# Attention with a third accumulating transfer per unit, keys loaded in halves, and a new order of work in the unit

## Chip, cores and metric

One core of a Trainium2 chip runs the whole program in one launch. The metric is the device time of the program in microseconds (us); lower is better. Before the change it is 3730.32 us, the median of three runs (3730.3 to 3734.2).

## What is computed

x is 8 x 1024 x 512 in float32. A conditioned transformer block is followed by a conditioned RMS norm:

```python
tp = (silu(time_emb) @ Wt + bt)[:, None, :]
shift_msa, scale_msa, gate_msa, shift_mlp, scale_mlp, gate_mlp = split(tp, 6)
h = layernorm(x, g1, be1) * (1.0 + scale_msa) + shift_msa
q, k, v = moveaxis((h @ Wqkv + bqkv).reshape(B, L, 3, H, HD), 2, 0)
attn = softmax(einsum('blhd,bmhd->bhlm', q, k) * HD ** -0.5)
h = einsum('bhlm,bmhd->blhd', attn, v).reshape(B, L, D) @ Wproj + bproj
x = x + gate_msa * h
h = layernorm(x, g2, be2) * (1.0 + scale_mlp) + shift_mlp
x = x + gate_mlp * (gelu(h @ W1 + b1) @ W2 + b2)
x = rmsnorm(x, rms_weight) * (1.0 + scale) + shift     # scale, shift from cond
```

There are 16 heads of width 32, and 1024 tokens in each of 8 batches.

## The kernel before

**Stages.** Stage 1 makes the normed input and the q, k and v rows and writes them to DRAM. Attention works in 64 **units**, u = 0 to 63. A unit is one batch, one group G = u // 2 of four heads (GH), and one half of the queries (512). Eight units make a batch. The MLP follows. This text is about attention, which lasts from about 571 to 2270 us of the span.

**A unit on the engines.** Softmax needs the row maximum before the exponential, so scores are made twice:
- `pe_maximum` (L736) makes scores with queries on the partitions, 128 queries x 512 keys a matmul, 32 for a unit (N_MAX). VectorE takes each one's maximum (`dve_maximum`, L1118). When a unit's 32 are done, `pe_send_max` (L745) turns them round, VectorE splits the negated maxima in two parts and SP's queue writes them into two spare rows of the q stack (`send_max`, L578).
- `pe_score` (L1299) makes the transposed scores, 128 keys x 512 queries, 32 for a unit: 8 key tiles kt x 4 heads. The maximum is subtracted inside the matmul, by the spare rows. ScalarE takes the exponential into the tile probs(u, kt) (L1445).
- `pe_values` (L1313) multiplies probs(u, kt) by v: four matmuls for a key tile, one a head, each on its own 32 columns of the array ("128*32" in the rows). The other matmuls here use the full array ("128*128").
- The softmax denominator is the sum of probs over all keys. The eight key tiles are first added into one, tile 4 of the unit, and four matmuls with ones (`pe_denominators`, L1327, also 128*32) sum over the partitions. Two of the adds are DMAs that GpSimd issues with accumulation (`pool_pair`, L1563: A adds tile 0 to tile 1, B adds 2 to 3). The other five are GpSimd tensor adds (`pool_add`, L1578).
- VectorE turns, inverts and spreads the denominator and scales the result (L1483 to L1506).
- 12 matmuls of the output projection of an earlier batch's tile (`pe_project_product`, L1344) are mixed in, from iteration u = 9 on (PROJ_LAG).

**What sets the order.** Two strings. `ORDER` is one iteration's list, read by every engine for its own letters:

```python
ORDER = ("sgsmmmssmsmaVlVsmsswmmsmsmmVVmsmssmmsmmsmssVV!s"
         "msmsmsmsmstrmspDVVmjmsjjjnmsmsjsmsjjsmsmjsmjjjj")
POOL_ORDER = "-1-3-6A-7B5"
```

s is a score, m a maximum (of unit u+1 before "!", of unit u+2 after it), V the values of one key tile, "!" the sending of unit u+1's maxima, D the denominator of unit u-1, t r p n VectorE's work on it, j a projection product, g, a and l the gate, split and low part of the projection, w the copy of the finished values. The first two V of an iteration are tiles 6 and 7 of the unit before (PV_LAG = 2), so the seventh is tile 4. Adjacent V and D are one **run** of 128*32 matmuls, since a, l, t, r, p, n and w are on other engines. Before the change an iteration has four runs: VV, VV, VV, DVV. `POOL_ORDER` is GpSimd's list: a digit is the tensor add of that key tile into tile 4, a letter a pair transfer, and "-" before either means that it is for unit u-1.

**Waits that matter.** D waits until the last add of unit u-1 is done (`pool_sum`). The first add of a unit, here 5, waits for tile 4's values, because it overwrites that tile. probs tiles 4 to 7 rotate through four buffers (ROTATING), so the exponential of tile 4, 5, 6 or 7 waits until tile 5, 6, 7 or 4 of the unit before has been added and read (`act_wait_for_buffer`). The first score of unit u waits for its maxima (`a_m`).

**Loads.** SP's queue carries, per iteration, q for unit u+2 (`load_q`, L560, 3 x 256 KB, and one small copy), the store of a gated tile (L1281), and the maxima. In even iterations it also carries keys for group G+1 (`load_keys`, L545, 3 x 512 KB, at the start) and values (`load_values`, L552, 512 KB, at the second V); in iteration 8b+2 the gates of a batch (L1275).

**Lead.** LEAD is the number of unit 1's maxima that are made in stage 1, since the iteration makes only those ahead of "!": 32 - 18 = 14.

## Time and profile before

| | |
|---|---|
| runs | 3734.2, 3730.32, 3730.3 us; median 3730.32 |
| the profiled execution | 3731.57 us, of which the span is 3729.7 |
| TensorE busy over the span | 3689.7 us, 99% |
| VectorE, ScalarE, GpSimd busy | 66%, 49%, 52% |
| granted TensorE clock | 0.999 |
| DMA moved | 480.41 MB |

The span is the time between the first and the last instruction of the profiled execution. Busy time is the time in which an engine executes; weight loads (PEld) overlap matmuls. The end of a matmul in these rows is modelled, so costs on TensorE are best read from the distance between starts. A row "x16" merges 16 records. The 128*32 matmuls in float32 leave two records each, so the values of one key tile are 8 records. Attention takes up slices 7 to 24 of the 40 that the page shows. "To landing" is the time from a transfer's issue until its semaphore is raised.

### The profile page before, as it was taken

Reading aid. Unit: us, or ns where it says so; the run is one execution under the profiler, and the core shown is the slowest. Engines: PE = TensorE matmul, PEld = TensorE weight load, DVE = VectorE, ACT = ScalarE, POOL = GpSimd, SP = SyncE. Lnnn points to the kernel's source line nnn. Section 1 sums busy time; section 2 is a strip of 40 time slices with the busy share of each in tenths; the row PEclk is TensorE's granted clock in tenths of the full one; section 3 lists DMA queues with packets and bytes.
Section 4 is the critical chain, followed back from the end, with each engine's and each line's share of the span. In section 5 each row is a group of like instructions: output and inputs, shape, how many; then the busy total and the mean of one; then the engine's idle time right before and its main releaser. Section 6 shows DMA issues by size and latency. Waiting matters only on the chain.

```text
span 3729.7 us, 50080 instructions
## 1 busy us (share of the span) xinstructions
PE 3689.7 (99%) x18430; PEld 2637.2 (71%) x18430; DVE 2444.4 (66%) x4107; ACT 1816.7 (49%) x3276; POOL 1957.8 (52%) x636
## 2 busy tenths in 40 slices
PE   8999999999999999999999999999999999999998
PEld 6788875455656565656556556888888888888887
DVE  6677668888988989889898983333443333434442
ACT  3222225666767676767676665333333333333333
POOL 1000116999999999999999996322231222222221
PEclk9999999999999999999999999999999999999999
DMA  8787776767776777677776764111111111111110
GB/s 285 246 270 241 244 246 137 154 143 164 164 171 150 164 160 174 151 157 162 171 160 151 165 147 143 43 44 61 46 37 46 37 46 37 46 37 46 37 46 23
DMA packets 219249, 480.41 MB, mean 129 GB/s; under 512 B 22931, under 2 KB 61843, under 8 KB 202755
## 3 DMA queue, kind: packets, MB, share of 16 engines
q1 hardware_dynamic: 200860, 345.08, 33.0%
q0 software_dynamic: 18144, 132.13, 17.2%
q8 instruction: 147, 2.41, 0.3%
q14 instruction: 98, 0.79, 0.1%
HBM read 225.36 MB, written 117.60 MB: 92 GB/s over the span
## 4 chain that ended last, share of the span: by engine, by line
PE 93%; POOL 3%; DVE 1%; issue 1%; ACT 1%; DMA 0%; SPq 0%; POOLq 0%; DVEq 0%; ACTq 0%
PE psum L736 12%; PE psum L1299 12%; PE psum L1313 12%; PE psum L595 10%; PE psum L597 10%; PE psum L596 10%; PE psum L1978 6%; PE psum L1974 6%; PE psum L1976 6%; PE psum L1344 4%; POOL probs_round L1578 2%; PE psum L1327 2%; PE psum L1927 1%; ACT probs L1445 0%; PE psum L745 0%
## 5 line engine op out<-in xcount | busy, mean ns | idle before, releaser
L1118 DVE TENSOR_REDUCE max_part<-psum 128x1 f32<-128x512 f32 x2048 | 1269.8, 679 | 68.4 <-PE psum L736 68.0
L1578 POOL TENSOR_TENSOR probs_round<-probs_round,probs_round 128x2048 f32<-128x2048 f32 x189 | 887.3, 4695 | 104.6 <-PE psum L1313 88.5
L2143 DVE TENSOR_TENSOR g_parts<-g_full,g_parts 128x512 fp32r<-128x512 f32 x256 | 259.3, 1013 | 805.5 <-ACT g_parts L2032 805.5
L1299 PE MATMUL psum<-q_stack,k_stack 128*128 128x512 f32 x2048 | 767.1, 400 | 0.8 <-ACT probs L1445 0.5
L736 PE MATMUL psum<-k_stack,q_stack 128*128 128x512 f32 x2048 | 755.0, 399 | 0.6
L1445 ACT ACTIVATE probs_round<-psum 128x512 f32<-128x512 f32 x1024 | 539.0, 603 | 329.8 <-PE psum L1299 327.1
L1445 ACT ACTIVATE probs<-psum 128x512 f32<-128x512 f32 x1024 | 544.0, 605 | 219.0 <-PE psum L1299 204.5
L1578 POOL TENSOR_TENSOR probs_round<-probs_round,probs 128x2048 f32<-128x2048 f32 x124 | 571.5, 4609 | 9.7
L2028 ACT ACTIVATE g_full<-psum,cols 128x512 f32<-128x512 f32 x256 | 176.6, 690 | 800.8 <-PE psum L597 800.4
L2239 POOL TENSOR_TENSOR y_out<-y_out,rows 128x512 f32<-128x512 f32 x60 | 77.3, 1288 | 853.0 <-DVE y_out L2178 853.0
L736 PEld LDWEIGHTS psum<-k_stack,q_stack 128*128 128x128 f32 x2048 | 383.8, 188 | 187.8 <-DVE max_part L1118 113.4
L1299 PEld LDWEIGHTS psum<-q_stack,k_stack 128*128 128x128 f32 x2048 | 384.4, 188 | 152.7 <-issue 59.3
L1974 PE MATMUL psum<-w_hi,g_parts 128*128 128x512 f32 x1024 | 401.2, 392 | 0.0
L595 PE MATMUL psum<-h_hi,w_hi 128*128 128x512 f32 x1024 | 399.8, 390 | 0.0
L1978 PE MATMUL psum<-w_hi,g_parts 128*128 128x512 f32 x1024 | 398.8, 389 | 0.0
L597 PE MATMUL psum<-h_hi,w_lo 128*128 128x512 f32 x1024 | 398.5, 389 | 0.0
L1976 PE MATMUL psum<-w_lo,g_parts 128*128 128x512 f32 x1024 | 398.4, 389 | 0.0
L596 PE MATMUL psum<-h_lo,w_hi 128*128 128x512 f32 x1024 | 398.4, 389 | 0.0
L1313 PE MATMUL psum<-probs,v_group 128*32 128x512 f32 x2048 | 246.7, 598 | 0.0
L1313 PE MATMUL psum<-probs_round,v_group 128*32 128x512 f32 x2048 | 245.5, 595 | 0.0
L595 PEld LDWEIGHTS psum<-h_hi,w_hi 128*128 128x128 f32 x1024 | 192.2, 188 | 43.2 <-issue 3.8
L1978 PEld LDWEIGHTS psum<-w_hi,g_parts 128*128 128x128 f32 x1024 | 192.2, 188 | 40.3
(193 smaller groups left out, 4949.9 us busy)
## 6 DMA issues: line engine op xcount, KB each, us to landing
probs<-probs POOLq DMA_DIRECT2D x126, 1024.0 KB, 7.7
qk_parts<-qk_out SPq DMA_DIRECT2D x128, 512.0 KB, 4.4
k_stack<-qk_parts SPq DMA_DIRECT2D x96, 512.0 KB, 7.0
q_stack<-qk_parts SPq DMA_DIRECT2D x192, 256.0 KB, 5.7
v_rows<-v_out SPq DMA_DIRECT2D x64, 256.0 KB, 3.8
v_group<-v_rows SPq DMA_DIRECT2D x32, 512.0 KB, 10.2
gated_attention<-gated SPq DMA_DIRECT2D x64, 256.0 KB, 4.7
x<-in_x SPq DMA_DIRECT2D x16, 1024.0 KB, 10.0
```

Of the source, the lines that this page charges most:

```text
L595: pe.matmul(dst, lh, rh, start=n == 0, stop=False)
L596: pe.matmul(dst, lh, rl, start=False, stop=False)
L597: last = pe.matmul(dst, ll, rh, start=False, stop=n == len(terms) - 1)
L736: pe.matmul(psum[:, bank, :], q_stack[u % 3][0:P, h, i * P:(i + 1) * P], k_stack[G % 2][0:P, h, kh * CH:(kh + 1) * CH], start=True, stop=T ...
L1118: dve.reduce_max(max_part[:, n:n + 1], psum[:, TURNS[at.turn][0], :], AX.X).then_inc(dve_smax, 1)
L1299: pe.matmul(psum[:, ST[n % 3], :], k_stack[G % 2][0:P, h, kt * P:(kt + 1) * P], q_stack[u % 3][0:P, h, :], start=True, stop=True).then_inc ...
L1313: i = pe.matmul(psum[h * HD:(h + 1) * HD, PV_BANK, :], v_group[G % 2][:, kt, h * HD:(h + 1) * HD], probs(u, kt)[:, h, :], start=kt == 0, s ...
L1445: act.activation(probs(u, kt)[:, h, :], psum[:, ST[n % 3], :], ACT.Exp, scale=SCALE).then_inc(act_exp, 1)
L1578: pool.tensor_tensor(total[:, :, :], total[:, :, :], probs(u, kt)[:, :, :], ALU.add).then_inc(pool_sum, 1)
L1974: pe.matmul(psum[:, ACC[m], :], gp[:, 0, cut], w2_hi[piece][:, at, :], start=i == 0, stop=False)
L1976: pe.matmul(psum[:, ACC[m], :], gp[:, 0, cut], w2_lo[piece][:, at, :], start=False, stop=False)
L1978: return pe.matmul(psum[:, ACC[m], :], gp[:, 1, cut], w2_hi[piece][:, at, :], start=False, stop=i == KM - 1)
```

## The change

`PAIRS` gets C = (6, 7): an accumulating transfer adds key tile 6 to 7, in place of the tensor add of tile 6. GpSimd's list becomes C of the unit before, 3 of the unit before, A, 7 of the unit before, B, 1, 5. It has four tensor adds and three transfers. Tile 1, the first add, now waits for tile 4's values. The exponential of tile 5 waits for C's landing, since it takes tile 6's buffer. Only the last two units add 6 and 7 with tensor adds, as before.

Keys load by halves of 512 (`load_keys(sp, G, half)`), each with a semaphore of its own. The second half loads at the start of an even iteration, behind q. The first half loads in the odd iteration before it, after 16 scores. The 32 maxima of a unit are now in the order of key halves (`max_place`), 16 of the first and then 16 of the second.

`ORDER` has three runs of 128*32 matmuls, VV, VV and VVDVV, and "!" comes after 10 maxima, so LEAD is 22.

```diff
-    ORDER = ("sgsmmmssmsmaVlVsmsswmmsmsmmVVmsmssmmsmmsmssVV!s"
-             "msmsmsmsmstrmspDVVmjmsjjjnmsmsjsmsjjsmsmjsmjjjj")
-    POOL_ORDER = "-1-3-6A-7B5"
+    ORDER = ("gsmssmmsmVVmwsmmsmssmmalVVs!smsmjssmmsjmssjmsmj"
+             "smsmsmsjsmsjmsmsmjsjmmVVDtrpnVVsmssmjmjsmsmjsmj")
+    POOL_ORDER = "-C-3A-7B15"
...
-    PAIRS = {"A": (0, 1), "B": (2, 3)}
+    PAIRS = {"A": (0, 1), "B": (2, 3), "C": (6, 7)}
...
+        MERGED = [PAIRS[which][1] for which in "AB"]
+        LAST_EARLY = [int(what) for what, before in POOL_STEPS
+                      if what.isdigit() and not before and int(what) not in MERGED]
+        LAST_LATE = [kt for kt in range(KT - ROTATING + 1, KT) if kt not in LAST_EARLY]
+        LAST_SUMS = LAST_EARLY + LAST_LATE
...
+        def max_place(n):
+            kh, rest = divmod(n, GH * TT)
+            return kh, *divmod(rest, TT)
...
-                pe.wait_ge(a_k[G % 2], 48 * (G // 2 + 1))
+            if h == 0 and i == 0:
+                pe.wait_ge(a_k[kh][G % 2], 48 * (G // 2 + 1))
...
-                if half == 0 and 0 < u and G + 1 < NGRP:
-                    sp.wait_ge(pe_st, u * 32)
-                    sp.wait_ge(pe_smax, ring_of_send(u - 1) + 1)
-                    load_keys(sp, G + 1)
                 if 0 < u and u + 2 < NU:
                     sp.wait_ge(pe_st, u * 32)
                     load_q(sp, u + 2)
+                if half == 0 and 0 < u and G + 1 < NGRP:
+                    sp.wait_ge(pe_smax, ring_of_send(u - 1) + 1)
+                    load_keys(sp, G + 1, 1)
...
+                    if what == "s":
+                        scores += 1
+                        if scores == N_MAX // 2 + 1 and half == 1 and G + 2 < NGRP:
+                            sp.wait_ge(pe_st, u * 32 + N_MAX // 2)
+                            sp.wait_ge(pe_smax, ring_of_send(u) + 1)
+                            load_keys(sp, G + 2, 0)
...
+                elif before == PAIRS["C"][0] and u < NU - 1:
+                    act.wait_ge(a_pair["C"], 16 * u)
...
+            elif kt == PAIRS["C"][1] and u < NU - 2:
+                pool.wait_ge(a_pair["C"], 16 * (u + 1))
```

How the instructions stand now is shown at three places. Numbers behind a name are buffers.

On TensorE, around the third V run of an iteration before the change (probs_119 and probs_120 are key tiles 2 and 3):

```order
L1299 MATMUL psum<-q_stack_106,k_stack_116 128x512 x2
L1313 MATMUL psum<-probs_119,v_group_125 32x512 x4
L1313 MATMUL psum<-probs_120,v_group_125 32x512 x4
L745 MATMUL psum<-ident,max_q 16x128
L1299 MATMUL psum<-q_stack_106,k_stack_116 128x512
```

and around its D:

```order
L1299 MATMUL psum<-q_stack_106,k_stack_116 128x512
L1327 MATMUL psum<-probs_round_122,ones 32x512 x4
L1313 MATMUL psum<-probs_round_123,v_group_125 32x512 x4
L1313 MATMUL psum<-probs_round_124,v_group_125 32x512 x4
L736 MATMUL psum<-k_stack_105,q_stack_108 128x512
```

The same two pieces now, with other line numbers (L1333 values, L1347 denominator, L749 maximum, L1319 score, L1364 projection):

```order
L1364 MATMUL psum<-wproj_lo,attn_hi_129 128x512
L749 MATMUL psum<-k_stack_105,q_stack_108 128x512 x2
L1333 MATMUL psum<-probs_119,v_group_125 32x512 x4
L1333 MATMUL psum<-probs_120,v_group_125 32x512 x4
L1347 MATMUL psum<-probs_round_122,ones 32x512 x4
L1333 MATMUL psum<-probs_round_123,v_group_125 32x512 x4
L1333 MATMUL psum<-probs_round_124,v_group_125 32x512 x4
L1319 MATMUL psum<-q_stack_106,k_stack_116 128x512
L749 MATMUL psum<-k_stack_105,q_stack_108 128x512
```

The two runs have become one of 20 matmuls, with the denominator in its middle, and the maxima's turn no longer stands behind the values of tiles 2 and 3.

On GpSimd, one iteration before (probs_round_122 is tile 4 of the unit, the sum; the rows are 5, 1, 3, 6, A, 7 and B):

```order
L1578 TENSOR_TENSOR probs_round_122<-probs_round_122,probs_round_123 128x2048
L1578 TENSOR_TENSOR probs_round_122<-probs_round_122,probs_118 128x2048
L1578 TENSOR_TENSOR probs_round_122<-probs_round_122,probs_120 128x2048
L1578 TENSOR_TENSOR probs_round_122<-probs_round_122,probs_round_124 128x2048
L1563 DMA probs_118<-probs_113 128x2048
L1578 TENSOR_TENSOR probs_round_122<-probs_round_122,probs_round_121 128x2048
L1563 DMA probs_120<-probs_119 128x2048
```

and now C, 3, A, 7 and B, then 1 and 5 of the next unit:

```order
L1585 DMA probs_round_121<-probs_round_124 128x2048
L1602 TENSOR_TENSOR probs_round_122<-probs_round_122,probs_120 128x2048
L1585 DMA probs_118<-probs_113 128x2048
L1602 TENSOR_TENSOR probs_round_122<-probs_round_122,probs_round_121 128x2048
L1585 DMA probs_120<-probs_119 128x2048
L1602 TENSOR_TENSOR probs_round_123<-probs_round_123,probs_118 128x2048
L1602 TENSOR_TENSOR probs_round_123<-probs_round_123,probs_round_124 128x2048
```

The add of tile 6 (probs_round_124) has become a DMA into tile 7's buffer (probs_round_121), ahead of the add of tile 3, and the add of tile 1 (probs_118) has moved behind B of its own unit.

On SP, an even iteration before (ahead of the maxima of the next unit):

```order
L545 DMA k_stack_116<-qk_parts 32x4x1024 x3
L560 DMA q_stack_106<-qk_parts 32x4x512 x3
L565 DMA q_stack_106<-q_stack_106 2x2048
L1281 DMA gated_attention<-gated_132 128x512
L552 DMA v_group_125<-v_rows 128x8x128
L578 DMA q_stack_108<-negmax_hi 1x16x128
L578 DMA q_stack_108<-negmax_lo 1x16x128
```

and now, beginning with the half of the keys that the odd iteration loads:

```order
L553 DMA k_stack_116<-qk_parts 32x4x512 x3
L568 DMA q_stack_106<-qk_parts 32x4x512 x3
L573 DMA q_stack_106<-q_stack_106 2x2048
L553 DMA k_stack_116<-qk_parts 32x4x512 x3
L1301 DMA gated_attention<-gated_132 128x512
L560 DMA v_group_125<-v_rows 128x8x128
L586 DMA q_stack_108<-negmax_hi 1x16x128
L586 DMA q_stack_108<-negmax_lo 1x16x128
```

The keys are two issues of half the size, one of them in the odd iteration, and q stands ahead of the other.

## Rows read from the trace of the kernel before

**Rows 1.** The page's heading, engines over the span, and DMA queues.

```profile
span 3729.7 us, 50080 instructions
PE 3689.7 (99%) x18430; PEld 2637.2 (71%) x18430; DVE 2444.4 (66%) x4107; ACT 1816.7 (49%) x3276; POOL 1957.8 (52%) x636
...
q0 software_dynamic: 18144, 132.13, 17.2%
...
probs<-probs POOLq DMA_DIRECT2D x126, 1024.0 KB, 7.7
```

**Rows 2.** Windows: an early iteration, twenty steady ones, and one alone; busy us by engine.

```profile
core 0: us, PE busy (x) PEld busy (x) DVE busy (x) ACT busy (x) POOL busy (x), PEclk, DMA share, GB/s
662.00:688.30 26.30, 24.80 (x139) 13.30 (x138) 22.34 (x40) 16.92 (x35) 24.66 (x8) 1.00 0.91 192
1378.00:1908.00 530.00, 530.00 (x2981) 318.01 (x2980) 475.82 (x821) 365.63 (x701) 493.64 (x141) 1.00 0.73 162
1428.00:1454.50 26.50, 26.50 (x153) 15.93 (x149) 23.80 (x42) 18.31 (x36) 24.65 (x8) 1.00 0.57 127
```

**Rows 3.** Timeline of PE, steady iteration: start us, us, engine, line, names, shape, count.

```profile
1426.76 0.61 PE L1299 MATMUL psum<-q_stack,k_stack 128*128 128x512 f32 x2
1427.30 1.92 PE L1313 MATMUL psum<-probs,v_group 128*32 128x512 f32 x16
1429.15 0.28 PE L745 MATMUL psum<-ident,max_q 128*16 128x128 f32 x1
...
1432.05 0.39 PE L1299 MATMUL psum<-q_stack,k_stack 128*128 128x512 f32 x1
1432.37 1.06 PE L1327 MATMUL psum<-probs_round,ones 128*32 128x512 f32 x8
1433.25 1.90 PE L1313 MATMUL psum<-probs_round,v_group 128*32 128x512 f32 x16
1435.08 0.50 PE L736 MATMUL psum<-k_stack,q_stack 128*128 128x512 f32 x1
1435.42 0.40 PE L1344 MATMUL psum<-wproj_hi,attn_hi 128*128 128x512 f32 x1
1435.65 0.39 PE L736 MATMUL psum<-k_stack,q_stack 128*128 128x512 f32 x1
...
1455.66 0.28 PE L745 MATMUL psum<-ident,max_q 128*16 128x128 f32 x1
```

**Rows 4.** Timeline of POOL, one early iteration.

```profile
654.57 4.60 POOL L1578 TENSOR_TENSOR probs_round<-probs_round,probs_round 128x2048 f32<-128x2048 f32 x1
659.12 0.86 POOL L1563 DMA_DIRECT2D probs<-probs  x1
659.73 4.87 POOL L1578 TENSOR_TENSOR probs_round<-probs_round,probs_round 128x2048 f32<-128x2048 f32 x1
664.26 1.17 POOL L1563 DMA_DIRECT2D probs<-probs  x1
...
680.86 4.59 POOL L1578 TENSOR_TENSOR probs_round<-probs_round,probs_round 128x2048 f32<-128x2048 f32 x1
```

**Rows 5.** Line L1563 (pairs A and B): time from issue to landing.

```profile
DMA to landing us min/median/max: 6.8/7.7/10.9
```

**Rows 6.** DMA queues while a pair and a plain load overlap, 2232 to 2237 us.

```profile
q0 software_dynamic: 117, 0.96, 91.9%
q1 hardware_dynamic: 114, 0.23, 13.9%
```

**Rows 7.** DMA queues from 1290 to 1320 us, one even iteration's loads and two pairs.

```profile
q1 hardware_dynamic: 959, 2.45, 38.0%
q0 software_dynamic: 288, 2.10, 34.1%
```

**Rows 8.** Timeline of DVE at the start of attention.

```profile
571.66 6.67 DVE L1118 TENSOR_REDUCE max_part<-psum 128x1 f32<-128x512 f32 x11
```

More of the change, by code:

```diff
@@ L291, in build_block @@
         act_hicopy, dve_alo = sem("act_hi_copy"), sem("dve_alo")
-        a_k, a_q, a_m, a_vg = sems("a_k", 2), sems("a_q", 3), sems("a_m", 3), sems("a_vg", 2)
+        a_k = [sems(f"a_k{half}_", 2) for half in range(NCH)]
+        a_q, a_m, a_vg = sems("a_q", 3), sems("a_m", 3), sems("a_vg", 2)
         a_z = sems("a_z", 3)
         a_gated, a_g = sems("a_gated", 2), sems("a_g", 2)
-        a_pair = {"A": sem("a_pair01"), "B": sem("a_pair23")}
+        a_pair = {"A": sem("a_pair01"), "B": sem("a_pair23"), "C": sem("a_pair67")}
         a_wr, act_w12, pool_w12 = sems("a_wr", 3), sem("act_w12"), sem("pool_w12")
@@ L365, in build_block @@
                 + [int(w) for w, before in POOL_STEPS if w.isdigit() and before])
-        MERGED = [to for _, to in PAIRS.values()]
-        LAST_SUMS = [kt for kt in SUMS if kt not in MERGED]
+        MERGED = [PAIRS[which][1] for which in "AB"]
[3 more added lines that the diff above has]
+        LAST_SUMS = LAST_EARLY + LAST_LATE
         def sums_done(u, kt):
@@ L545, in load_keys @@
                 sp.dma_start(
[L546 to L548 removed]
+                    k_stack[G % 2][n * HD:(n + 1) * HD, :, cut].bitcast(fp32),
+                    qk_dram[b, part, at:at + P, cut].rearrange("(h d) t -> d h t", h=GH)
+                ).then_inc(a_k[half][G % 2], 16)
         def load_values(sp, G):
@@ L722, in pe_maximum @@
             G = u // NCH
[L723 to L724 removed]
+            kh, h, i = max_place(n)
             if n == 0:
@@ L1258, in sp_attention @@
                     load_gates(sp, b)
-                values = 0
+                scores = values = 0
                 for what in ORDER:
-                    if what == "!":
+                    if what == "s":
[4 more added lines that the diff above has]
+                            load_keys(sp, G + 2, 0)
+                    elif what == "!":
                         send_max(sp, u + 1)
@@ L1849, in pool_tail @@
             pool_project(pool, LEFT[1])
-            for what, before in POOL_STEPS:
-                if before and int(what) not in MERGED:
-                    pool_add(pool, NU - 2, int(what))
+            for kt in LAST_LATE:
+                pool_add(pool, NU - 2, kt)
             pool_residual_part(pool, 0, 0)
```

21 lines of the change are left out of this document (11 added, 10 removed).

## The prediction

> **What bounds the kernel now.** I read the busy shares over the span, then the windows inside attention, then the order of starts on TensorE in one iteration, then GpSimd's timeline, then the transfers. TensorE is busy for 99% of the span [rows 1]. In a stretch of twenty steady iterations it is busy for all 530.00 us, GpSimd for 493.64, VectorE for 475.82 [rows 2]. So a steady iteration is as long as TensorE's list: from one turn of maxima (L745) to the next, 1455.66 - 1429.15 = 26.51 us [rows 3]. The iterations before u = 9 have no projection. There TensorE is busy for 24.80 of 26.30 us [rows 2], and the period, 680.86 - 654.57 = 26.29 us, is GpSimd's [rows 4]. Two limits, then: TensorE in 54 iterations (9 to 62), GpSimd in 8 (1 to 8). Stage 1 and the MLP are not touched.
>
> **What a run of 128\*32 matmuls costs.** On the full array, starts lie 0.23 us apart (1435.42 to 1435.65). The first matmul of D starts 0.32 after the one before it: 0.09 more. Two V last from 1427.30 to 1429.15, 1.85 us. D and two V last from 1432.37 to 1435.08, 2.71. One more key tile is thus 0.86, and a fixed 0.13 is left of each run. The first full matmul after a run is followed at 0.34 in place of 0.23: 0.11 more. Entering and leaving costs 0.09 + 0.13 + 0.11 = 0.33 us a run [rows 3]. The work in the runs stays the same: nine groups of four matmuls.
>
> **The change, part by part.**
>
> *Three runs for four.* The matmuls are the same in number and shape, and one boundary goes: 0.33 us in each of 54 iterations, **-17.8 us**. The long run lasts 5 x 0.86 + 0.13 = 4.4 us without a maximum or a score. VectorE's cover is the maxima that wait in banks (about 0.6 us each, from 6.67 us for 11 [rows 8]) and the denominator's four steps, which D in the middle of the run sets free. It had 26.5 - 23.8 = 2.7 us to spare an iteration [rows 2], and 2.4 are left. ScalarE has 8.
>
> *GpSimd's list.* It loses one tensor add (4.6 us from start to the next instruction) and gains one issue of 0.6 (659.12 to 659.73) [rows 4]. What matters is the loop that closes on itself: D, values of tile 4, the tensor adds, D of the next unit. Before: 2 x 0.86 + 5 x 4.65 + A's issue 0.6 = 25.6, against 26.3 measured, so semaphores take 0.7. Now there are two ways round. Through GpSimd alone: 1.7 + 4 x 4.65 + 2 x 0.6 + 0.7 = 22.2. Through C, whose landing add 7 waits for: 1.7 + adds 1 and 5, 9.3, + C from issue to landing, L, + add 7, 4.65, + 0.7 = **16.4 + L**. The steady iteration (26.2) hides this as long as L is below 9.8. Pairs land in 7.7 at the median, between 6.8 and 10.9 [rows 5].
>
> *What L is.* Places in an iteration are counted here from `ORDER`, with the costs above. Tile 4's values end 4.8 us before the iteration does (16 full matmuls, one V and the boundary), and adds 1 and 5 take 9.3, so C is issued 4.5 us into the next iteration. In an odd iteration only q is ahead. In an even one SP has just issued q, half the keys and a store, 1.8 MB; plain loads run at 2.45 MB in 11.4 us (38.0% of 30) [rows 7], so 8.3 us of work, of which 4.9 are left when C is issued. The nearest row on sharing is a stretch in which both queues have work: 117 pair packets and 114 plain ones, 91.9% of the time for the pair and 13.9% for the load [rows 6]. They take turns packet by packet, and the pair's packets are the long ones. A pair of 5.1 us (34.1% of 30 for two [rows 7]) grows by 15%, to L = 8.5. The other bound is that the loads are served first: 7.7 + 4.9 = 12.6. I take 9.5, nearer to the row. The Trainium skill, page "DMA: Bandwidth & Descriptors", section "Anatomy of one DMA — SWDGE (gpsimd) path", gives such a transfer 2.0 us plus its bytes over 436e3; for 1 MB that is an estimate of 4.4, C would never be last, and the sum below would have -23 in place of -10. The trace does not agree (7.7).
>
> *Early iterations.* TensorE's list there is 26.5 - 12 x 0.23 - 0.33 = 23.4; the loop through C is 24.1 in odd ones (7.7) and 25.9 in even ones (9.5), mean 25.0. Against 26.3 that is 1.3 us in each of 8: **-10.4**. Bounds: 23.4 in all (-23), nothing (0).
>
> *ScalarE's new wait.* The exponential of tile 5 waits for C. Its first score stands about 14.1 us into the iteration, C lands at 4.5 + 9.5 = 14.0, and three more scores fit into the banks, 1.5 us. Nothing, up to L of about 10.5. Without this cover it would be the same late C as above, not a second cost.
>
> *Keys by halves, maxima by halves.* Same bytes, half of them moved to the odd iteration. The first half has about 20 us before its use, the second about 15. SP issues three transfers more in two iterations and waits at the 17th score, with nothing urgent behind it. Nothing.
>
> *Maxima sent earlier.* "!" moves from about 14 to 8.4 us, so their transfer has 18 us in place of 12. It also has more in front of it (second rival). Nothing.
>
> *LEAD 14 to 22.* Eight more maxima ahead of the first score, at the rate of VectorE, which is already behind there (11 in a row [rows 8]): 8 x 0.6 = 4.8. The last iteration has eight fewer, at TensorE's rate, 1.8. Net **+3.0**, between 0 and 5.
>
> *Sum.* -17.8 - 10.4 + 3.0 = -25.2. The profiled execution took 3731.6, which gives 3706.4; the median of the runs is 1.3 below it, which gives 3705. I say **3706**. A difference of under 0.2% (7.5 us) is about what a measurement of this kernel can't tell from no change.
>
> **The rivals.**
>
> *C is late, and the kernel slower.* The place is add 7 of an even iteration, with D and tile 5's exponential behind it; the price is L - 9.8 in 31 even iterations. It decides above L = 10.6, where 31 x 0.8 = 25 eats the gain. For it: transfers fill the 16 DMA engines for 0.73 x 26.5 = 19.3 us an iteration [rows 2], a third pair makes it 24.4 of 26.2, or 93%; the longest landing is already 10.9 [rows 5]; a pair's first packet must get past 4.9 us of loads. Against it: the taking of turns [rows 6]. With L = 11.5: 31 x 1.7 = 53, so 3759; served behind the loads, 12.6: 3793. Most of the doubt is here.
>
> *The maxima are late in the gate iterations.* Plain transfers get only 14% of the time while a pair runs [rows 6]. Ahead of the maxima in an even iteration stand q, keys, store and values, 2.3 MB or 10.7 us; with C and A it is 10.7 + 10.2 + 1 = 22 us, in time for 26.2. Seven iterations add 256 KB of gates, 1.2 us, and then pair B comes in front (issued at about 20): 2 to 3 us late. 7 x 2.5 = 17, so 3723: no difference to speak of. The Trainium skill, same page, section "Queues, rings and completion order", has each DMA engine take turns between the queues packet by packet; the counts 117 and 114 agree with that, and it is this rule by which the plain queue, not the pair, would be the one to suffer.
>
> *The long run costs what it saves.* VectorE or ScalarE runs dry in it and the banks fill unevenly afterwards, so TensorE waits 0.33 an iteration elsewhere. Only the early gain is left: 3731.6 - 7.4 = 3724.
>
> *C lands as quickly as 7.7 everywhere* and early iterations run at TensorE's 23.4: 3731.6 - 17.8 - 23 + 3 = 3694.
>
> *It does not do what it says.* The order shows the one run in place of two and the DMA in place of the add, so this is left out.
>
> **How the numbers follow.** Forecast 0.50 (3694 to 3716), C late 0.27, late maxima 0.10, the long run 0.08, the quick case 0.05. Faster by over 0.2%: 0.50 + 0.05 + a share of the two middle ones = 0.60. Slower: 0.25, since C can be late by little. Within 0.2%: 0.15. The range goes from the quick case, 3694, to a C late by about 1.7 us, 3757.
>
> **What would show it.** Right: three runs an iteration, turns of maxima 26.2 us apart from u = 9 on and about 25 before; C landing within 10 us; no wait of D on GpSimd. Wrong: even iterations longer than odd ones, add 7 waiting for a DMA for more than about 3 us, scores waiting for the maxima's transfer in every eighth iteration, or VectorE idle and then late after the long run.

## The result and the profile after

The change made the kernel slower: 3761.58 us at the median (3759.95 to 3763.03, four runs) against 3730.53 (3730.3 to 3734.2, four runs) before, a ratio of 1.008 with a 95% interval of 1.0067 to 1.0093. The profiled execution took 3761.82 us. The forecast of 3706 and its range up to 3757 both missed it, on the side of the first rival. Two executions at a far lower granted clock are left out of all figures below, one of the experiment "Four runs" (10933 us, clock 0.344) and one of the kernel before (4085 us, 0.851).

Page of the changed kernel: heading, engines, chain, the costliest groups of GpSimd and the pairs. It answers to [rows 1].

```profile
span 3760.0 us, 50240 instructions
...
PE 3696.4 (98%) x18430; PEld 2638.2 (70%) x18430; DVE 2459.0 (65%) x4107; ACT 1830.9 (49%) x3276; POOL 1723.4 (46%) x636
...
PE 77%; DMA 10%; POOL 9%; issue 2%; DVE 1%; ACT 1%; POOLq 0%; SPq 0%; ACTq 0%; DVEq 0%
...
L1602 POOL TENSOR_TENSOR probs_round<-probs_round,probs_round 128x2048 f32<-128x2048 f32 x127 | 583.1, 4592 | 200.0 <-DMA probs_round<-probs_round 194.6
...
probs<-probs POOLq DMA_DIRECT2D x126, 1024.0 KB, 8.6
...
probs_round<-probs_round POOLq DMA_DIRECT2D x62, 1024.0 KB, 8.5
```

GpSimd lost 234 us of work, as meant. But pair C ("probs_round<-probs_round") is on the chain of work that ended last with its transfer, and GpSimd stood idle for 194.6 us before its tensor adds (L1602) until C landed.

Waits of the changed kernel (engine, line, waited for: us in total, times, longest):

```profile
POOL probs_round L1602 <- DMA probs_round<-probs_round: 194.6, 62, 6.2
...
ACT probs_round L1467 <- DMA probs_round<-probs_round: 44.4, 30, 2.3
...
PE psum L1319 <- ACT probs_round L1467: 31.4, 30, 1.9
...
PE psum L1347 <- POOL probs_round L1602: 1.5, 5, 0.3
```

TensorE's own waits stand at the scores (L1319), behind ScalarE's exponential. At D (L1347) it waits for GpSimd's adds 1.5 us in all. The chain through an even iteration shows the same (start, us, what): C lands at 1281.13, the exponential of tile 5 begins, and 0.65 us after it a score.

```profile
1269.44 11.69 DMA probs_round<-probs_round
...
1281.21 0.61 ACT probs_round L1467
...
1281.86 0.50 PE psum L1319
```

C's median landing, 8.5 us, lies between the 7.7 that I had for odd iterations and the 9.5 for even ones. It says nothing here, because the two kinds differ: 7.2 us at the median in odd iterations, 11.3 in even ones (up to 12.4). Turns of maxima (L758 now) on TensorE, an odd iteration between the first two, an even one between the next two:

```profile
1246.77 0.27 PE L758 MATMUL psum<-ident,max_q 128*16 128x128 f32 x1
1273.10 0.27 PE L758 MATMUL psum<-ident,max_q 128*16 128x128 f32 x1
1300.95 0.27 PE L758 MATMUL psum<-ident,max_q 128*16 128x128 f32 x1
```

The odd one takes 26.3 us, the even one 27.9. Steady even iterations take 27.1 to 30.1 over the kernel. Against 26.29, the 26 of them are 40.2 us too long together. The four early even ones are 9 us longer than the 25.05 of the early odd ones. The window over twenty steady iterations (columns as in [rows 2]) shows the gap on TensorE, which before was busy for all 530.00 [rows 2]:

```profile
1378.00:1908.00 530.00, 520.41 (x2902) 313.63 (x2904) 467.02 (x803) 364.40 (x688) 407.97 (x137) 0.99 0.91 196
```

What happens at the start of an even iteration is seen on two queues. SP, then GpSimd, 1264 to 1286 us:

```profile
1264.35 1.28 SPq L568 DMA_DIRECT2D q_stack<-qk_parts  x3
...
1266.35 1.39 SPq L553 DMA_DIRECT2D k_stack<-qk_parts  x3
...
1268.26 0.43 SPq L1301 DMA_DIRECT2D gated_attention<-gated  x1
1268.73 1.55 SPq L560 DMA_DIRECT2D v_group<-v_rows  x1
```

```profile
1269.44 0.86 POOL L1585 DMA_DIRECT2D probs_round<-probs_round  x1
...
1281.28 4.57 POOL L1602 TENSOR_TENSOR probs_round<-probs_round,probs_round 128x2048 f32<-128x2048 f32 x1 [5.51 <-DMA probs_round<-probs_round]
```

Every load of the iteration is issued before C, at 1269.44. The DMA queues of the same kernel from 1269.5 to 1273.5, just behind that issue (packets, MB, share of the 16 engines' time), with the row of the load issued last (KB, us to landing):

```profile
q1 hardware_dynamic: 496, 0.90, 105.8%
...
v_group<-v_rows SPq DMA_DIRECT2D x1, 512.0 KB, 18.2
```

The pair's queue, q0, has no row: not one of its packets ran in these 4 us, though in a quiet stretch its first would have come at 1270.9. GpSimd's issue itself took 0.86 us, as it does in odd iterations. And from 1275.5 to 1280, when the pair runs and the maxima's rows and the rest of the values are beside it:

```profile
q0 software_dynamic: 121, 0.91, 96.9%
q1 hardware_dynamic: 126, 0.06, 6.9%
```

Here the counts are about equal, as they were in [rows 6]. By the packets of the trace, C's first one came 4.98 us after the issue in place of 1.45 in a quiet stretch, and its last 11.0 after. GpSimd's add waited 5.51 us for it.

The values are an exception. They were issued 0.7 us before C, and yet 930 of the 1056 packets of 512 bytes (1024 of values, 32 of maxima's rows) ran after C's first one, so they landed only after 18.2 us. The queries, keys, gates and store, in packets of 2048 bytes, were through but for 15.

### The profile page after: what moved, and what is told of

It is laid out like the page before. It is cut to its first block, busy times and chain, and to the rows that moved or that the text cites. A ratio compares the mean times of both kernels' runs of the same rounds, so it can differ in the third digit from the quotient of the medians.

```text
span 3760.0 us, 50240 instructions
## 1 busy us (share of the span) xinstructions
PE 3696.4 (98%) x18430; PEld 2638.2 (70%) x18430; DVE 2459.0 (65%) x4107; ACT 1830.9 (49%) x3276; POOL 1723.4 (46%) x636
## 4 chain that ended last, share of the span: by engine, by line
PE 77%; DMA 10%; POOL 9%; issue 2%; DVE 1%; ACT 1%; POOLq 0%; SPq 0%; ACTq 0%; DVEq 0%
PE psum L603 10%; PE psum L604 10%; PE psum L605 10%; DMA probs_round<-probs_round 9%; POOL probs_round L1602 9%; PE psum L1333 8%; PE psum L1319 7%; PE psum L749 7%; PE psum L2001 6%; PE psum L1997 6%; PE psum L1999 6%; PE psum L1364 3%; PE psum L1347 2%; PE psum L1950 1%; ACT probs_round L1467 0%
## 5 line engine op out<-in xcount | busy, mean ns | idle before, releaser
L1319 PE MATMUL psum<-q_stack,k_stack 128*128 128x512 f32 x2048 | 779.8, 408 | 33.3 <-ACT probs_round L1467 31.4
L749 PE MATMUL psum<-k_stack,q_stack 128*128 128x512 f32 x2048 | 758.9, 396 | 1.5 <-DVE max_part L1133 0.7
L1602 POOL TENSOR_TENSOR probs_round<-probs_round,probs_round 128x2048 f32<-128x2048 f32 x127 | 583.1, 4592 | 200.0 <-DMA probs_round<-probs_round 194.6
L1602 POOL TENSOR_TENSOR probs_round<-probs_round,probs 128x2048 f32<-128x2048 f32 x124 | 588.8, 4748 | 31.3 <-issue 27.8
L1319 PEld LDWEIGHTS psum<-q_stack,k_stack 128*128 128x128 f32 x2048 | 383.7, 187 | 277.4 <-issue 110.9
L749 PEld LDWEIGHTS psum<-k_stack,q_stack 128*128 128x128 f32 x2048 | 385.5, 188 | 129.9 <-DVE max_part L1133 60.2
L1333 PE MATMUL psum<-probs,v_group 128*32 128x512 f32 x2048 | 248.3, 602 | 0.0
L1333 PE MATMUL psum<-probs_round,v_group 128*32 128x512 f32 x2048 | 245.8, 595 | 0.0
```

The source lines that it names most:

```text
L749: pe.matmul(psum[:, bank, :], q_stack[u % 3][0:P, h, i * P:(i + 1) * P], k_stack[G % 2][0:P, h, kh * CH:(kh + 1) * CH], start=True, stop=T ...
L1319: pe.matmul(psum[:, ST[n % 3], :], k_stack[G % 2][0:P, h, kt * P:(kt + 1) * P], q_stack[u % 3][0:P, h, :], start=True, stop=True).then_inc ...
L1333: i = pe.matmul(psum[h * HD:(h + 1) * HD, PV_BANK, :], v_group[G % 2][:, kt, h * HD:(h + 1) * HD], probs(u, kt)[:, h, :], start=kt == 0, s ...
L1602: pool.tensor_tensor(total[:, :, :], total[:, :, :], probs(u, kt)[:, :, :], ALU.add).then_inc(pool_sum, 1)
```

## The experiments

All kernels compute the whole program; where copies are added, the text says so. Times are medians in us with the ratio to the kernel before on the same chip; before was 3730.98 to 3731.85 in these sessions.

### Moving the loads away from C

**Keys behind the sending.** The second key half is issued behind the maxima's rows, where C is already running.

```diff
-                if half == 0 and 0 < u and G + 1 < NGRP:
-                    sp.wait_ge(pe_smax, ring_of_send(u - 1) + 1)
-                    load_keys(sp, G + 1, 1)
...
                         send_max(sp, u + 1)
+                        if half == 0 and 0 < u and G + 1 < NGRP:
+                            load_keys(sp, G + 1, 1)
```

> The changed kernel, with the second half of the keys (3 x 256 KB, even iterations) issued behind the maxima's transfer instead of at the start of the iteration. Bytes, matmuls and adds are the same. Theory 1, order in the queues: a pair that is issued while plain loads are queued gets its first packet only when they are through, so C lands 10.5 to 12 us after its issue in even iterations, which are 27.1 to 30 us long where odd ones are 26.3. With 3.5 us of loads less in front of it C lands at about 9 and nearly all of the even excess (40 us in 26 steady iterations, 9 in the early ones) goes: 3718 to 3726. Theory 2, share: the 16 DMA engines are 91% busy, and any third pair is late wherever it stands: 3757 to 3765. Theory 3, the long run of 20 column matmuls starves VectorE or ScalarE: no difference, 3760.

3714.97 (3714.68 to 3715.8), ratio 0.9955 [0.9937, 0.9973], some 3 us faster than theory 1 gave. Turns of maxima, window of the twenty steady iterations and landings of all pairs in this kernel:

```profile
1281.60 0.27 PE L758 MATMUL psum<-ident,max_q 128*16 128x128 f32 x1
1307.90 0.27 PE L758 MATMUL psum<-ident,max_q 128*16 128x128 f32 x1
```

```profile
1378.00:1908.00 530.00, 529.77 (x3006) 323.25 (x3005) 479.83 (x827) 373.25 (x705) 422.84 (x142) 1.00 0.94 203
```

```profile
DMA to landing us min/median/max: 6.8/8.4/11.6
```

Steady iterations are 26.30 us, nearly without exception, and early ones about 25.0. GpSimd still waits 108.9 us for C, but C lands after 8.5 us at the median in even iterations and no longer holds them. The DMA engines are *more* loaded (0.94 against 0.91), so it was not the load as such. This kernel is 46.6 us faster than the change and 17 faster than before.

**Values in the odd iteration.** The keys stay, the values move behind the first key half.

```diff
-                        if values == PV_LAG and half == 0 and G + 1 < NGRP:
...
+                        if values == PV_LAG and u == 0:
+                            load_values(sp, 1)
...
+                        if scores == N_MAX // 2 + 1 and half == 1 and 0 < G and G + 1 < NGRP:
+                            sp.wait_ge(pe_pv, KT * (u - 1))
+                            load_values(sp, G + 1)
```

> The changed kernel, with the load of the values (512 KB in 512-byte packets, 1.8 us of DMA time) moved from the second V of even iterations to the odd iteration before, behind the first half of the keys. Keys and everything else stay. Theory 1, order in the queues: C's first packet comes 1.3 us earlier in even iterations, L near 9.5, and two thirds of the excess go: 3728 to 3742. Theory 2, share, and theory 3, the long run: 3757 to 3765.

3750.18 (3746.09 to 3751.44), 1.0048 [1.0032, 1.0063]: a gain of 11 us, where theory 1 gave 20 to 34 and the others none. Even iterations range from 26.4 to 30.1, and adds wait 177.3 us for C. Without the values C's first packet still comes at 3.3 to 5.8 us in steady even iterations, 4.0 at the median. That fits the row of the values above: most of their packets had not stood ahead of C.

**Both moved.**

> Both moves together: only q and a gated store stand before C in every iteration. Same bytes, same share of the DMA engines (about 92%). Theory 1: C lands in 8 to 8.5 us in every iteration, even iterations are as long as odd ones (26.3 from u = 9 on, 25 before), and the total is 3712 to 3718, faster than both kernels. Theory 2 and theory 3: 3757 to 3765, since neither the bytes nor the order on TensorE changed.

3715.83 (3714.38 to 3716.83), 0.9957 [0.9941, 0.9973], as expected. Steady iterations are 26.30 but for a few (up to 26.83), GpSimd waits 77.9 us for C; no better than the keys alone.

**Gates moved too**, to the middle of the odd iteration.

> The kernel with keys and values moved, and the gate rows (0.5 MB broadcast to 128 partitions, every eighth iteration) moved from the start of an even iteration to the middle of the odd one as well. Theory (iterations already run at 26.30, since pair C lands before 9.8 us everywhere): nothing is left to win, 3714 to 3717 us. Rival (gate iterations still cost something at their start): up to 3 us less, 3711 to 3713.

3716.27 (3714.59 to 3717.16), 0.9958 [0.9944, 0.9973]. Nothing was left to win, since C no longer held any iteration.

### Order or bytes?

**Copies at the start of odd iterations.** To "both moved", three copies of 0.26 MB are added ahead of C; they go to memory that nothing reads.

```diff
+                if half == 1 and 2 < u:
+                    if u > 6:
+                        sp.wait_ge(a_ballast[G % 2], 48 * ((G - 1) // 2))
+                    for n in range(3):
+                        sp.dma_start(ballast_dram[G % 2, n],
+                                     qk_dram[b, 0, n * P:(n + 1) * P, 0:CH]
+                                     ).then_inc(a_ballast[G % 2], 16)
```

> This is the kernel with keys and values moved (3715.8 us, every late iteration 26.30) plus a dose: three copies of 128x512 float32 each (0.79 MB together, the size of a q load), issued by SyncE at the start of each odd iteration from 3 to 61, about 5 us before pair C is issued. Theory (plain loads that are queued ahead of a pair are served to the end before its first packet): in odd iterations C's first packet moves from 1.4 us behind the issue to 3.5 to 5 us, its landing from 6.7 to 9.5 to 11, and those iterations grow to 26.5 to 28 us; even ones stay at 26.30. With 29 odd iterations, 3725 to 3750 us. Rival 1 (it is the pair's own length or the clock that made the change slow, the loads ahead of it don't matter): first packet stays at 1.4 us and the time at 3716. Rival 2 (turns packet by packet): first packet stays at 1.4 to 2 us, the landing becomes 8 to 9.5 us and the time 3716 to 3720.

3715.96 (3714.03 to 3716.75), 0.9956 [0.994, 0.9973]. My theory's numbers were wrong here, and those of the second rival, turns packet by packet, fit: in odd iterations C's first packet came at 1.8 us and its landing at 8.3 at the median, and the iterations stayed at 26.3. In the iteration with C issued at 1278.26, its first packet could have come at 1279.7 and came at 1280.34. The queues from 1279.7 to 1280.3:

```profile
q1 hardware_dynamic: 116, 0.21, 96.9%
```

The pair again has no row, but it is held for only 0.6 us. The dose was too small to tell the theories apart by time.

**Twice the copies**, six at the same place.

> The kernel with keys and values moved, with six copies of 0.26 MB at the start of each odd iteration from 3 to 61 where three left the time at 3716.0 (they were through 0.6 us behind the time at which C could have started, C landed at 8.1 us, under the 9.8 that are hidden). Three copies took about 3 us of all engines, so six end about 3 us later. Theory (loads issued first are served to the end): C's first packet at 4.5 to 5.5 us in odd iterations, landing 10 to 11.5, those iterations 26.9 to 28.2, even ones 26.3; 3730 to 3770 us. Rival (turns packet by packet, a load's packet of 2048 bytes against one of 8192 of the pair): C starts at 1.5 to 2 us and lands at 7.5 to 9, and the time stays at 3716 to 3720.

3754.75 (3753.17 to 3755.27), 1.0062 [1.0045, 1.0079]. That is the loss of the change, made by loads that have nothing to do with it. Pairs' landings (minimum, median, maximum), then the queues from 1239.5 to 1242, with C issued at 1237.96:

```profile
DMA to landing us min/median/max: 6.9/9.6/13.5
```

```profile
q1 hardware_dynamic: 275, 0.51, 91.6%
```

C's first packet came 4.2 us after its issue (at 1242.16), its last after 10.6, and in the two odd iterations after that the first after 3.1, with the last after 10.0 and 10.5. Over all odd iterations with copies the first came after 1.6 to 4.2, 3.1 at the median, less than the 4.5 to 5.5 expected, and C landed after 11.4 at the median. Most odd iterations took 26.9 to 28.3, some stayed at 26.3. Taking turns was expected to give 1.5 to 2 us and 3716 to 3720.

**The dose and the price.** From a landing of about 10.1 us on, each microsecond by which C is later costs one. In the changed kernel C landed after 10.93, 11.69 and 12.07 us in three iterations of 27.10, 27.86 and 28.25 us; here after 10.76, 11.79 and 12.14 in three of 26.93, 27.95 and 28.33. Each time the iteration is 26.3 us plus the landing less 10.1, to within 0.04. With the late keys a landing of 10.02 left one at 26.28. Of the steady iterations with a landing above 10.25 in the change, in this kernel and in "values in the odd iteration", 53 of 67 lie within 0.05 us of this line.

**The same three copies behind the sending**, with C already running.

> The same copies of 0.79 MB in the same odd iterations, but issued behind the sending of the maxima, where pair C is already running. The same bytes lie between the issue of C and the step that waits for it. Theory (order of issue decides): C's first packet stays at 1.4 us, the copies share the engines with its second half, landing 7.5 to 10 us, all late iterations stay at 26.30 to 26.4 and the time at 3715 to 3720. Rival (the bytes beside the pair count, wherever they stand): odd iterations as long as with the copies at the start.

3731.9 (3728.45 to 3735.0), 1.0001 [0.9992, 1.001]. This was not expected either. In the odd iteration C is not the one that suffers: from 1296.5 to 1302, with pairs running, the copies issued at 1295.80 get almost nothing, and they run when the pair is through:

```profile
q0 software_dynamic: 125, 1.02, 101.7%
q1 hardware_dynamic: 81, 0.12, 7.0%
```

```profile
q1 hardware_dynamic: 951, 1.39, 102.2%
```

The second row is 1303.5 to 1308.5. By then SP has keys and values behind the copies. Pair B, issued at 1305.73, gets its first packet after 4.0 us, and 0.94 MB of loads run in these 4.0 us. 795 of the packets are of 512 bytes, from values issued 3.3 us before B. The loss shows in the iterations that follow: even ones take up to 29.1 us with C landing after up to 12.9, and maxima wait 7.8 us in all for queries. So the queue that holds the engines keeps them, and the other side pays afterwards.

**All loads held until C is issued.** The change with one more wait; no byte added or moved to another stretch.

```diff
                     sp.wait_ge(pe_st, u * 32)
+                    if half == 0:
+                        sp.wait_ge(pool_sum, sums_done(u - 1, 5))
                     load_q(sp, u + 2)
```

> The changed kernel with one added wait: in even iterations SyncE holds its loads (queries, second key half, gates, values, in their old order) until GpSimd's fourth addition of the unit before is done, which is when GpSimd issues pair C. The loads and their bytes are the same, and nothing is taken from the stretch; only the order of issue turns round, the loads coming some 5 us later. Theory (what is issued first is served first, nearly alone): C's first packet falls from 4.7 to 5.3 us behind its issue to 1.5, its landing from 10.5 to 12.4 to 6.6 to 7.5 us, even iterations fall to 26.3 (25.0 early), and the time to 3714 to 3720 us; the loads trickle beside the pairs and land 10 us or more later. If the maxima's rows, issued behind these loads, then come too late for the next scores, TensorE waits at its scores and the time is up to 20 us more. Rival (the bytes in the stretch count, not their order): C lands as late as before, and the time stays at 3755 to 3765.

3978.87 (3977.64 to 3980.27), 1.0664 [1.0648, 1.068]: far outside what either side gave. One part came nearly as expected. C, issued at 1415.76, had its first packet after 2.2 us and its last after 8.5, in place of 5 and 11. It landed after 9.1, though, where 6.6 to 7.5 was expected. The queues from 1417.5 to 1424, then from 1424 to 1427:

```profile
q0 software_dynamic: 129, 1.05, 83.1%
q1 hardware_dynamic: 222, 0.42, 20.1%
```

```profile
q1 hardware_dynamic: 419, 0.77, 103.4%
```

The turn round moved the damage to two others. Pair A, issued at 1420.89, behind the held loads, got its first packet 6.15 us later. And the queries crept beside C. I had watched the maxima's rows and forgotten that the maxima of the next unit need these queries at once. TensorE:

```profile
1426.24 0.77 PE L749 MATMUL psum<-k_stack,q_stack 128*128 128x512 f32 x1 [6.32 <-DMA q_stack<-qk_parts]
1426.81 0.63 PE L1321 MATMUL psum<-q_stack,k_stack 128*128 128x512 f32 x1
```

An even iteration takes about 35 us in place of 27.8. For C's first packet this run answers with order: 2.1 us at the median in even iterations in place of 4.9. It can't show what that is worth, since another wait is longer, and as a remedy it is useless.

### The other parts of the change

**Four runs.** "Both moved", with the long run cut in two.

```diff
-             "smsmsmsjsmsjmsmsmjsjmmVVDtrpnVVsmssmjmjsmsmjsmj")
+             "smsmsmsjsmsjmsmsmjsVVjmmDtrpnVVsmssmjmjsmsmjsmj")
```

> The kernel of both moves, with the long run cut in two again: the two V of key tiles 2 and 3 stand three full matmuls earlier, so an iteration has four runs, VV, VV, VV and DVV. Theory of the prediction: each run costs 0.33 us, in 54 iterations bound by TensorE: 18 us slower than the kernel of both moves, iterations 26.6. Rival: a run costs nothing that is not hidden, and the two are the same within 3 us.

3737.15 (3735.61 to 3738.04), 1.0014 [1.0005, 1.0024]; steady iterations 26.66 (1421.58, 1448.22, 1474.88 are turns), early ones about 25.4. One run costs 0.36 us in every iteration, 21 us in all.

**No third pair.** The change with the tensor add of tile 6 back, and the old list "-1-3-6A-7B5" for GpSimd.

> The changed kernel with its new order, its key halves and its loads where the change put them, but without C: key tile 6 is a tensor add again and GpSimd's list is the old one (1, 3, 6, A, 7 of the unit before or of this one, B, 5). Theory 1 (late C is the whole loss): even and odd iterations are alike, 26.3 to 26.4 from u = 9 on, and the early ones are back at GpSimd's 26.3. Against the kernel with C on time (3715) that is 8 x 1.3 = 10 us more: 3723 to 3730. Rival: the third transfer is what makes the new order possible, and D then waits for GpSimd in every iteration: 3760 or more.

3736.82 (3735.98 to 3739.41), 1.0015 [1.0005, 1.0024], above the 3723 to 3730 expected and far below the rival. Steady iterations are 26.53, not 26.30. Waits from 1378 to 1908 us, GpSimd's and ScalarE's:

```profile
POOL probs L1583 <- ACT probs_round L1465: 22.9, 20, 1.1
```

```profile
ACT probs_round L1465 <- POOL probs_round L1598: 51.3, 20, 2.6
```

Once in each iteration GpSimd waits for ScalarE, and once ScalarE for GpSimd. GpSimd is busy for 24.7 us of 26.5 with its five adds. On TensorE one score in the iteration I looked at starts 0.13 us late and the next 0.11, which is the 0.23 that is missing. That the two engines form a loop as long as the old iteration is read from these waits, and no run shows it by itself. The new order gains nothing without C, and C is what pays for the missing run.

**Key halves alone.** Order and GpSimd's list as before, no C.

> The kernel before with one part of the change, the keys and the maxima by halves (half of the keys loaded in the odd iteration); order of the unit and GpSimd's list as before, no C. The prediction costs this at nothing: 3727 to 3733. Rival: the halves or the other order of the maxima cost or give something of their own, over 5 us.

3736.85 (3733.41 to 3740.51), 1.0013 [1.0003, 1.0022]: 5 us lost. Most iterations are 26.52, some even ones 27.5 to 27.8. GpSimd there:

```profile
1616.77 0.87 POOL L1583 DMA_DIRECT2D probs<-probs  x1
...
1621.91 1.18 POOL L1583 DMA_DIRECT2D probs<-probs  x1
...
1635.50 4.61 POOL L1598 TENSOR_TENSOR probs_round<-probs_round,probs 128x2048 f32<-128x2048 f32 x1 [1.55 <-DMA probs<-probs]
```

A key half is issued at 1617.37, behind pair A, is served when A is through, and holds pair B, issued at 1621.91, until 1626.5. It is the same mechanism without C. TensorE pays at D here: 20.3 us of waits for the adds in the profiled execution, which was the slowest of ten (3740.5).

**C in the old order**, with GpSimd's list "-1-C-3A-7B5".

> The kernel before with the halves and with C in place of the tensor add of tile 6 (GpSimd's list 1, C, 3, A, 7, B, 5), order of the unit as before, with D at 17 us of the iteration. Theory 1: in even iterations C is issued behind loads, lands late, and D stands 2.4 us earlier than in the new order: several us lost in each even iteration, 3800 to 3880; early odd iterations gain, to about 25. Rival (C is cheap, only the new order is at fault): 3718 to 3730.

3870.43 (3868.47 to 3873.17), 1.0371 [1.0355, 1.0386]. That is inside the 3800 to 3880 expected. Steady even iterations take 28.1 to 32.6 us, odd ones 26.5 to 28.1, and GpSimd waits for C for up to 5.2 us. C lands no later than in the change (10.7 us at the median of even iterations), but here TensorE stops at D:

```profile
PE psum L1347 <- POOL probs_round L1602: 101.4, 37, 3.6
```

This is the path that the prediction gave to a late C. D stands earlier in the old order, and in the new one the scores stop first. The granted clock also fell, to 0.987 over the span.

**Turn of maxima directly behind the run**, on top of the late keys, since after the change it stands between full matmuls.

```diff
-    ORDER = ("gsmssmmsmVVmwsmmsmssmmalVVs!smsmjssmmsjmssjmsmj"
+    ORDER = ("gsmssmmsmVVmwsmmsmsmmsalVV!ssmsmjssmmsjmssjmsmj"
```

> The kernel of e1 with the turn of the maxima (a matmul on 16 columns) moved from behind the first score after a V run to directly behind the run. In e1 it stands between two full matmuls: 0.34 us before it and 0.32 after the one that follows, so it seems to be a small run of its own; in the kernel before it stood directly behind a run. Theory: that is the 0.11 us by which iterations (26.30) miss the forecast 26.18, and it goes: 7 us faster than e1, 3708. Rival: VectorE has not finished the 32nd maximum by then, so TensorE waits 0.2 to 0.4: 3722 to 3740.

3725.72 (3724.23 to 3727.77), 0.9984 [0.9974, 0.9993], 11 us worse than the late keys alone, as its rival had it. TensorE here:

```profile
1414.80 1.92 PE L1332 MATMUL psum<-probs,v_group 128*32 128x512 f32 x16
1416.84 0.27 PE L758 MATMUL psum<-ident,max_q 128*16 128x128 f32 x1
```

The turn starts 2.04 us after the run where it took 1.85 before the change [rows 3]: 0.19 us of waiting, and 26.50 an iteration in place of 26.30.

**The same with the maxima pulled ahead** ("VVmwsmmmmsmsssalVV!smsmj").

> The kernel with the late key half (3715.0) with the last maxima pulled ahead of scores (VVmwsmmmmsmsssalVV!smsmj in place of VVmwsmmsmssmmalVVs!smsmj), so that VectorE has done the last maximum when the V run ends, and with the turn of the maxima directly behind that run. Theory (a 16-column turn between full matmuls costs 0.11 us more than behind a run, and with the turn there TensorE waited 0.19 us for VectorE): steady iterations fall from 26.30 to about 26.2 and the time to 3706 to 3712. Rival (VectorE is still not done, since it stands behind the gating and not behind the last maximum): 3725 as with the turn behind the run and the old maxima. Rival 2 (four maxima in a row wait for VectorE, 571 ns each against 227 on TensorE): the wait shows at the maxima and the time is 3718 to 3730.

3754.6 (3753.34 to 3755.65), 1.0062 [1.0047, 1.0077]. None of the three expectations held. The turn no longer waits, but iterations are 27.0 to 27.1. VectorE waits from 1378 to 1908 us:

```profile
DVE attn_lo L1545 <- ACT psum L1416: 20.6, 20, 1.0
```

Once in each iteration VectorE stands still for 1.0 us for ScalarE's copy, with the maxima queued behind it. Rival 2's direction was right, its size too small. Which of the waits sets the 27.0 was not taken apart.

## Why the prediction was wrong

**The step that failed is "What L is".** It took 9.5 us in even iterations from the taking of turns, and 12.6 as the bound "the loads are served first". Measured were 10.6 to 12.4, 11.4 on average. [Rows 6] were read rightly for what they are: equal counts of packets while a pair *already* runs (121 to 126 in the changed kernel too). I carried them over to the opposite case, where loads are running when the pair is issued. There the pair gets nothing until nearly all of them are through (496 packets to none). The end of the queries, keys, gates and store set the first packet, and the 4.9 us that I had worked out for the loads still ahead was the delay seen: first packets 4.0 to 5.7 us after the issue, 4.9 at the median. The bound was too high because it added the 4.9 to a whole landing. The first 1.45 us of a landing pass beside the loads, and 7.7 + 4.9 - 1.45 is 11.2.

The Trainium skill, page "DMA: Bandwidth & Descriptors", section "Queues, rings and completion order", has each DMA engine take turns between queues packet by packet. If its packets are those of the profile, the trace agrees while a pair runs and disagrees when loads are ahead of it. Why the pair's turn does not come there, no run shows. How early a load must be issued to stand ahead is not shown either: values issued 0.7 us before C mostly ran beside and after it, values issued 3.3 us before a pair B mostly ran before it. A pair's issue on GpSimd is not what got slower, since it took 0.85 to 0.89 us for every C.

**A second step failed with it: "ScalarE's new wait".** It was put at nothing up to an L of about 10.5, and a late C was to be paid at add 7 and D, above 9.8. Measured, TensorE waits 31.4 us at the scores behind tile 5's exponential and 1.5 at D. The cover ends at 10.1 (26.3 us + L - 10.1 in three kernels). The price was nearly the same by either path, so the 3759 of the first rival came out almost right for a partly wrong reason.

Step by step:

- *Three runs for four, -0.33 us:* confirmed; the run put back cost 0.36. The iteration became 26.30 and not 26.18, though. Before the change the turn of maxima stood directly behind a run and cost nothing: it and the score after it took 0.35 us, which a single matmul takes there (0.34 behind D's run).

```profile
1429.15 0.28 PE L745 MATMUL psum<-ident,max_q 128*16 128x128 f32 x1
1429.19 0.48 PE L1299 MATMUL psum<-q_stack,k_stack 128*128 128x512 f32 x1
1429.50 0.40 PE L736 MATMUL psum<-k_stack,q_stack 128*128 128x512 f32 x1
```

  Now it stands one matmul later. In the kernel with late keys:

```profile
1281.26 0.50 PE L1318 MATMUL psum<-q_stack,k_stack 128*128 128x512 f32 x1
1281.60 0.27 PE L758 MATMUL psum<-ident,max_q 128*16 128x128 f32 x1
1281.63 0.48 PE L1318 MATMUL psum<-q_stack,k_stack 128*128 128x512 f32 x1
1281.95 0.39 PE L749 MATMUL psum<-k_stack,q_stack 128*128 128x512 f32 x1
```

  From the turn to the matmul behind the next score it is again 0.35, but here a score alone would take 0.23. That is about 0.11 in 54 iterations, 6 us, under "maxima sent earlier: nothing". It is read from distances only; both kernels that put the turn back lost more elsewhere. The kernel with four runs and the turn in its new place agrees: 26.66 where the old one had 26.51.
- *GpSimd's list, 16.4 + L against 26.2:* not what held the steady iterations, since D hardly waited. It is what holds the old order, where TensorE waits 101.4 us at D. The run without the third pair showed a wait between GpSimd and ScalarE that I had left out.
- *Early iterations, 25.0 on average:* odd ones 25.05 where 24.1 was forecast, even ones 27.0 to 27.7 for 25.9, since L failed; about 25.05 everywhere once the loads moved. The 25.0 was partly luck. With the loads moved, the chain there goes from the values of tile 4 over adds 1, 5 and 3 to an exponential and back to TensorE's list, a loop that the prediction did not have.
- *Keys by halves, nothing:* wrong by 5 us when alone, through pair B.
- *LEAD, +3.0:* no run has it by itself. In the traces the first score comes 46.7 us after the first maximum in place of 43.2, so 3.5 for the 4.8 at the start, and the iteration before the last is 0.9 shorter for the 1.8.
- *Sum:* 3706.4 + 6 (turn) + 40.2 + 9 (late C) = 3761.6, against 3761.8 profiled. That it meets so closely is luck in part: the same sum without the late C gives 3712.4, and the kernel with late keys was profiled at 3715.8.

Not all of the 40.2 is C's own. In two even iterations, of 30.0 and 30.1 us, C landed after 12.4 and 12.1, which gives 28.6 and 28.2. The rest, 3.2 us together, goes with a lower clock (last section).

**The rivals.** The first was right in time and nearly in size: 3759 for L = 11.5. Its chance of 0.27 was too small, because a row from one direction was counted as evidence for the other. Maxima that come late for the scores do not appear among the waits. A long run that costs what it saves is excluded by the four-run kernel.

**The parts together.** Halves with the new order but without C are 3737, halves alone 3737, halves with C in the old order 3870, all three 3762. All three with one key half issued 9 us later are 3715, the fastest kernel here. Counted from each unit's first score to the next, before against that kernel: the eight early iterations give back 9.2 us (forecast 10.4), the other 54 give back 13.1 (forecast 17.8, less the 6 of the turn), and 6.6 are lost, 4.1 ahead of unit 0, 0.7 in iteration 0 and 1.8 behind the last. The span falls by 15.7.

## What to carry to other kernels

Before a transfer is put on the path that sets the time, ask what stands *ahead* of it on the DMA engines when it is issued, not how much moves beside it. Plain loads have slack, so issue them behind the urgent transfer, but look who comes next: loads held back until one pair is on its way stood ahead of the following pair, and their own reader waited. Read how two queues share in both orders of arrival, and look at odd and even iterations apart: the median landing of all pairs was 8.6 us in the slow kernel and 8.4 in the fast one. Find out which engine's wait stops the busiest one. Here GpSimd stood idle for C for 194.6 us, but the time was lost through ScalarE.

## What the runs showed of the hardware

- **Two DMA queues do not share evenly in time.** With an accumulating pair running (packets of 8192 bytes), plain loads got 6.9% to 20% of the time. With loads running, a pair issued behind them had its first packet up to 5.7 us after its issue in the changed kernel (6.2 with the loads held back), in place of 1.45.
- **The clock fell behind a wait of TensorE.** With the loads held back, most full matmuls after a wait of 6.3 us started 0.43 us apart until 1431, then 0.23 again. The window of that kernel shows the granted clock, 0.74 on average over these 13 us, so for a part of it 1.2 GHz in place of 2.4:

```profile
1418.00:1431.00 13.00, 6.68 (x26) 4.39 (x19) 4.92 (x10) 4.18 (x8) 8.59 (x3) 0.74 1.06 236
```

  From 1426.24 to 1431.03 there are 11 starts, 4.8 us where 2.5 are usual, so the slower clock added 2.3 us to the wait. In the changed kernel it fell twice in attention, each time within 1.5 us after a score that had waited 1.84 or 1.86 us (at 1661.56 and 1497.84), in the two iterations of 30 us:

```profile
1499.20:1502.50 3.30, 3.30 (x13) 1.32 (x15) 1.99 (x4) 0.66 (x3) 2.62 (x1) 0.50 0.61 137
```

  The wait of 1.13 us in the iteration shown at 1281.86 left it at full speed, and so did others of up to 1.77 us.
